# Two-layer attention and expert kernel: first attention's first diagonal chunk masked behind the exponentials instead of by mask products

## Chip, cores and metric

The kernel runs on one core of one Trainium2 chip. The metric is the time of one execution on the device, in microseconds (us); lower is better. The core's engines are named as in the profile: PE is TensorE, DVE is VectorE, ACT is ScalarE, POOL is GpSimd, SP is SyncE, which here only issues DMAs. PE, DVE, ACT and POOL each work through their own list of instructions in order and meet at semaphores.

## What is computed

The input x is 8 sequences of 256 tokens of 128 channels. Two blocks follow each other for every sequence:

```
x = layernorm(x + attention_A(x))           # 16 heads of 8 channels, one shared key and value head, rotary, causal
h = x + attention_B(rmsnorm(x, g1))         # 16 query heads of 64 channels, 4 key and value heads, rotary, causal
y = h + experts(rmsnorm(h, g2))             # router, top 2 of 8 experts, capacity limit
x = layernorm(x + y)
```

The change touches attention A. Its core, for one sequence:

```
att = einsum('bthd,bThd->bhtT', q, k) / sqrt(8)
att = where(T > t, -inf, att)               # a key later than the query counts nothing
att = softmax(att, axis=-1)
out = einsum('bhtT,bThd->bthd', att, v)
```

## The kernel before, in words

**Stages and steps.** Each sequence goes through eight stages (PA project A, MA row maxima A, SA scores and values A, TA finish A, PB project B, MB maxima B, SB scores and values B, TB finish B). The main loop runs steps s = -4 to 7. In a step each engine does one piece of every stage that is active, for different sequences: stage SA of sequence n is done in step s = n - 3 (`AHEAD`, L80), so SA is active in steps -3 to 4. PB is active in steps -2 to 5, SB from step 0, TB from step 1. The order of the work inside a step is written out by hand, once per engine: PE in `step` (L969), DVE in `step` (L1335), ACT in `step` (L1785), POOL in the loop at L586, the DMA issuer in the loop at L483. After the last step come the experts.

**PSUM.** Scores go to `ps_st` (two halves of 1024 columns). Everything else that PE makes goes through `ps_r`, a ring of four banks: PE takes the next bank with `fill` (L648), which waits until the reader of its previous content has freed it; the order is the list `ORDER` (L70).

**Scores of attention A.** The 256 x 256 causal square of a sequence is cut into three 128 x 128 chunks with keys on the partitions and queries along the row: DIAG0 (first keys, first queries), OFF, DIAG1. Each is done for all 16 heads, 2048 columns. `scores_a(s, c)` (L684) makes chunk c in four column groups of 512. For a diagonal chunk it first lays the mask into PSUM with four products of the identity and `kmask` (L696; -1e30 where the key is later than the query), then adds the four products of keys and queries (L699). Two exponentials on ACT (`exp_a`, L1684, the instruction at L1689) write the probabilities to `pt`: DIAG0 and DIAG1 to the same part, `pt_a(kind)` (L413), OFF to another. `values_a(s, qt)` (L704) multiplies probabilities and values (L714); `values_a(s, 0)` takes DIAG0 alone and waits for its two exponentials through `probs_a`. The row maximum that keeps the exponentials small comes from stage MA (masks at L661, products at L784, maxima on DVE at L1193, turned by PE at L791, negated by ACT at L1736, carried as a row by a DMA at L481); it is not touched.

**What stands around it in a step of PE:** B's projection `project(s, 0)` (L956), `scores_a(s, 0)`, A's maxima 10 and 11 (L661, L784), B's values (L929), the turned maxima (L791), B's weights (L945), B's maxima 8 to 11 (L661, L908), `project(s, 1)` (L956), the turned maxima of B (L916), A's input turned (L669), `values_a(s, 0)` (L714), `project_a` (L750, L755), the router's turned tokens (L812), `scores_a(s, 1)` (L699).

**DVE beside it:** B's rotary products of the first half, `rotate(s, 0)` (L1305 to L1309), A's maxima 10 and 11 (L1193), then, where TB is active, four small Newton steps for an inverse root (`newton`, L1155 to L1161) and two normalising products (L1392), B's maxima 8 to 11 (L1193), `rotate(s, 1)`, `rotate_a` (L1231 to L1239).

**POOL:** where TB is active two products on `oT` at the start of the step (L591), then `add_rotary(s, 0)` and `add_rotary(s, 1)` (three adds each, L554; each waits for DVE's bank to be freed, and DVE's later rotary writes wait for them), `spread_a` (L538 to L546), a copy of B's values (L610) and of the tokens (L621).

Of the kernel before, what the change touches and what calls it, by code (L numbers as in the profile page):

```python
# [27 lines left out]
ALU = mybir.AluOpType  # L28
# [3 lines left out]
P = 128  # L32
# [3 lines left out]
H = 16  # L36
# [25 lines left out]
DIAG0, OFF, DIAG1 = 0, 1, 2  # L62
# [17 lines left out]
AHEAD = {"PA": 4, "MA": 3, "SA": 3, "TA": 2, "PB": 2, "MB": 1, "SB": 0, "TB": -1}  # L80
# [10 lines left out]
def stages(step):  # L91

    return {x for x, a in AHEAD.items() if 0 <= step + a < NB}
# [82 lines left out]
E_A, E_B = len(CHUNKS_A), len(CHUNKS)  # L176
# [3 lines left out]
RG = P // 4  # L180
# [7 lines left out]
def build(nc, x, Wq, bq, Wk, bk, Wv, bv, Wo, bo, g1, g2, wq, wk, wv, wo, router_w, router_b,  # L188
          w1, w2, w3, cf, cb, out):
    with ExitStack() as ctx:  # L190
# [15 lines left out]
        def sem(name):  # L206
            return ctx.enter_context(nc.semaphore(name))
# [173 lines left out]
        free = [sem(f"free{b}") for b in range(RING.banks)]  # L381
        sc_a, sc_b = sem("sc_a"), sem("sc_b")
        probs_a, probs_b = sem("probs_a"), sem("probs_b")
        xn_in = sem("xn_in")
        prod_in = sem("prod_in")
        rot_in = sem("rot_in")
# [26 lines left out]
        def pt_a(kind):  # L413
            return pt[:, 2 + kind % 2]
# [12 lines left out]
        def emptied(eng, s, name):  # L427

            eng.wait_ge(free[RING.bank(s, name)], RING.freed(s, name) + 1)
# [89 lines left out]
        def _(pool):  # L519
# [13 lines left out]
            def spread_a(n):  # L533

                pool.wait_ge(chain_k, n + 1)
                both = qkr_a[:, :, 0:QA].rearrange("p t (h d) -> p t h d", d=DA)
                high = hr[:, :, :].bitcast(F32).rearrange("p t (h d) -> p t h d", d=DA)
                nc.gpsimd.tensor_tensor(qz[:, :, :, 2 * DA:3 * DA], both[:, :, 0:H, :], high[:, :, 0:H, :],  # L538
                                        ALU.subtract)
                for i in range(2):  # L540
                    nc.gpsimd.tensor_copy(qz[:, :, :, DA * i:DA * (i + 1)], high[:, :, 0:H, :])
                places = kz[:, :, :].rearrange("p t (a r) -> p t a r", a=4)
                one, hi_k = (x[:, :, H:, :].broadcast_to([P, NT, 4, DA]) for x in (both, high))
                for i in (0, 2):
                    nc.gpsimd.tensor_copy(places[:, :, :, DA * i:DA * (i + 1)], hi_k)
                nc.gpsimd.tensor_tensor(places[:, :, :, DA:2 * DA], one, hi_k, ALU.subtract).then_inc(kz_in, 1)  # L546

            def add_rotary(s, t):

                for i in range(3):  # L550
                    emptied(pool, s, f"p{t}{i}")
                    w = 512 if i < 2 else HKV * DB
                    part = qkr[:, t, 512 * i:512 * i + w]
                    nc.gpsimd.tensor_tensor(part, part, prod[:, (3 * t + i) % 2, 0:w], ALU.add).then_inc(add_in, 1)  # L554

            def scatter(i, lo, hi, src):

                pool.wait_ge(sc_in, i + 1)
                pool.wait_ge(z_dma, 48)
                for k in range(lo, hi):  # L560
                    if 1 < k < PASSES[0][1]:
                        pool.wait_ge(sc_dma[k % 2], 16 * (k // 2))
                    nc.gpsimd.indirect_dma_start(xs_dram[:, :], bass.IndirectOffsetOnAxis(sidx[:, k:k + 1], 0),
                                                 src[:, k - lo, :], None).then_inc(sc_dma[k % 2], 16)

            def load_slots(i):

                for a in range(2):
                    pool.wait_ge(sc_dma[a], 8 * PASSES[i][1])
                for k, (lo, hi) in enumerate(CHUNKS_X[i]):  # L570
                    nc.gpsimd.dma_start(xe[i][:, lo - START[i]:hi - START[i], :], rows(xs_dram, lo, hi)) \
                        .then_inc(xe_in[i][k], 16)

            def keep_inputs(lo, hi, src):

                for k in range(lo, hi):
                    ins = nc.gpsimd.tensor_tensor(src[:, k - lo, :], src[:, k - lo, :],
                                                  wx[:, k:k + 1].broadcast_to([P, C]), ALU.mult)
                ins.then_inc(keep_in, 1)
# [6 lines left out]
            for s in range(FIRST, NB):  # L586
                on, u, m = stages(s), s % 2, s - 1
                if "TB" in on:
                    pool.wait_ge(b_dma, 32 * s)
                    for k in range(HKV // 2):  # L590
                        ins = nc.gpsimd.tensor_tensor(  # L591
                            oT[:, k], pvb[1 - u][:, k, :, :].rearrange("p t (g c) -> p t g c", g=G), oT[:, k], ALU.mult)
                    ins.then_inc(oT_in, 1)
                if "PB" in on:
                    add_rotary(s, 0)
                    add_rotary(s, 1)
                if "PA" in on:
                    spread_a(s + AHEAD["PA"])
                if s == FIRST:
                    for z in range(2):  # L600
                        nc.gpsimd.memset(kdiag[z][:, :, :, :].bitcast(F32), 0.0).then_inc(zeroed, 1)
                    nc.gpsimd.memset(zeros, 0.0).then_inc(zx_in, 1)
                    pool.wait_ge(c_in, C_IN)
                    nc.gpsimd.tensor_copy(nrow[:, :, :].rearrange("p h (t c) -> p (h t) c", t=NT),
                                          kmask.unsqueeze(1).broadcast_to([P, H * NT, P])).then_inc(prep, 1)
                if "PB" in on:
                    pool.wait_ge(add_in, 6 * (s + 2) + 6)
                    if "SB" in on:
                        pool.wait_ge(full, RING.full(s, "sm1"))
                    nc.gpsimd.tensor_copy(vb[u][:, :, :, :].rearrange("p t k d -> p t (k d)"), qkr[:, :, QB:]) \  # L610
                        .then_inc(v_in, 1)
                if s == ROUTED[0]:
                    pool.wait_ge(xfa_in, NB0)
                    scatter(0, *PASSES[0], xf_all)
                    load_slots(0)
                if s == NB - 1:
                    pool.wait_ge(share_in, 1)
                    keep_inputs(*PASSES[0], xf_all)
                if "TB" in on:
                    pool.wait_ge(xf_in, m + 1)  # L620
                    nc.gpsimd.tensor_copy(xf_all[:, NT * m:NT * (m + 1), :], xf[:, :, :]).then_inc(xfa_in, 1)  # L621
# [23 lines left out]
        def _(pe):  # L645
# [38 lines left out]
            def scores_a(s, c):  # L684

                n = s + AHEAD["SA"]
                kind = KINDS_A[c]
                kt, qt = BLOCKS[kind]
                if n or c:
                    pe.wait_ge(probs_a, E_A * n + 2 * c)  # L690
                if c == 0 and s >= 0:
                    pe.wait_ge(probs_b, E_B * (s + 1))
                pe.wait_ge(r_dma[qt], 16 * (n + 1))
                o = [ps_st[:, a // 2, a % 2, :].rearrange("p (h t) -> p h t", h=4) for a in range(4)]
                for a in range(4) if kind != OFF else ():
                    nc.tensor.matmul(o[a], ident_b, kmask.unsqueeze(1).broadcast_to([P, 4, P]), start=True, stop=False)  # L696
                for a in range(4):
                    rows = slice(RG * a, RG * a + NROW + 1)
                    mm = nc.tensor.matmul(o[a], kta[rows, a, P * kt:P * (kt + 1)], qta[rows, :, P * qt:P * (qt + 1)],  # L699
                                          start=kind == OFF, stop=True, tile_position=(RG * a, 0))  # L700
                    if a % 2:
                        mm.then_inc(sc_a, 1)

            def values_a(s, qt):  # L704

                n = s + AHEAD["SA"]
                o = fill(s, f"av{qt}")
                if qt == 0:
                    emptied(pe, s - 1, "qkv")
                pe.wait_ge(probs_a, E_A * n + (2 if qt == 0 else E_A))  # L710
                blocks = [(DIAG0, 0)] if qt == 0 else [(OFF, 0), (DIAG1, 1)]
                for i, (kind, kt) in enumerate(blocks):
                    for a in range(4):
                        mm = nc.tensor.matmul(o[RG * a:RG * (a + 1), :], va[n % 2][:, kt, :],  # L714
                                              pt_a(kind)[:, 4 * a:4 * a + 4, :], start=i == 0,
                                              stop=i == len(blocks) - 1, tile_position=(0, RG * a))
                mm.then_inc(full, 1)
# [251 lines left out]
            def step(s):  # L969
# [51 lines left out]
                if "SA" in on:  # L1021
                    scores_a(s, 0)
# [26 lines left out]
                if "SA" in on:  # L1049
                    scores_a(s, 1)  # L1050
# [863 lines left out]
```

## Time and profile before

| what | value |
|---|---|
| median of 3 runs | 586.88 us (585.63 to 587.46) |
| profiled execution, its own time | 582.76 us |
| its span, first to last instruction | 580.9 us |
| PE busy | 483.3 us, 83% of the span |
| DVE busy | 386.6 us, 67% |
| ACT busy | 229.6 us, 40% |
| POOL busy | 161.6 us, 28% |
| mean granted TensorE clock | 0.940 of full speed |

Engine times are busy times and overlap each other. The rows further down come from the same profiled execution; their times count from the start of its span. In a row of the timeline the columns are the start in us, the duration in us (of all the instructions that the row merges), the engine, the line, the operation, output and inputs with their shapes, the count, and in brackets the idle time of the engine just before it with what ended it.

### The profile page before, as it was taken

The page shows a single profiled execution, that of the slowest core. Times are in us where ns is not written, and L with a number is a line of the kernel's source. Part 1 is how long each engine was busy: PE and PEld are TensorE (multiplying, and loading weights), DVE is VectorE, ACT ScalarE, POOL GpSimd, SP SyncE. Part 2 cuts the span into 40 slices and gives each one's busy share as a digit, 9 for nine tenths or more (in the row PEclk, how much of TensorE's full clock was granted, in tenths as well). Part 3 has the DMA queues.
Part 4 walks back from the last instruction along what each step waited for, and adds up shares of the span by engine and source line. Part 5 has one row for each costly group of instructions (what it writes and reads, how often), then busy time and mean ns, then how long its engine had stood idle before and what let it go on. Part 6 is the DMA issues. An engine that isn't in the chain of part 4 may idle for free.

```text
span 580.9 us, 8112 instructions
## 1 busy us (share of the span) xinstructions
PE 483.3 (83%) x2788; PEld 266.4 (46%) x2788; DVE 386.6 (67%) x1096; ACT 229.6 (40%) x420; POOL 161.6 (28%) x200
## 2 busy tenths in 40 slices
PE   3776886899989989998999899999878689898920
PEld 2333453454354535544563555355354336565610
DVE  3518879657758675777668576766877544675785
ACT  1241442454383346425432742464133132445400
POOL 4210602400413230324202330403406542043531
PEclk9877997899999999999999999999979899999965
DMA  7400000000011003000300030030070332023223
GB/s 210 156 1 2 2 0 1 3 1 1 3 38 38 1 4 75 1 1 3 73 2 2 3 73 3 2 74 1 15 207 20 101 77 73 2 60 100 70 54 86
DMA packets 19093, 23.82 MB, mean 41 GB/s; under 512 B 2630, under 2 KB 15374, under 8 KB 18158
## 3 DMA queue, kind: packets, MB, share of 16 engines
q1 hardware_dynamic: 15308, 18.19, 11.8%
q0 software_dynamic: 1648, 4.07, 2.5%
q10 hardware_dynamic: 2098, 1.05, 0.6%
q8 instruction: 23, 0.38, 0.3%
q14 instruction: 16, 0.13, 0.1%
HBM read 16.71 MB, written 6.28 MB: 40 GB/s over the span
## 4 chain that ended last, share of the span: by engine, by line
PE 57%; DVE 19%; ACT 11%; issue 5%; DMA 4%; POOL 3%; ACTq 1%; POOLq 0%; DVEq 0%; SPq 0%
PE ps_r L929 7%; PE ps_st L894 6%; ACT pt L1689 5%; PE ps_r L803 4%; PE ps_r L661 4%; PE ps_st L883 4%; PE ps_r L956 4%; DVE rmax L1193 3%; PE ps_r L714 3%; DMA pt<-ys_dram,gidx 3%; PE ps_r L945 3%; PE ps_r L784 3%; DVE rmax_a L1193 2%; POOL qkr L554 2%; PE ps_st L1095 2%
## 5 line engine op out<-in xcount | busy, mean ns | idle before, releaser
L554 POOL TENSOR_TENSOR qkr<-qkr,prod 128x512 f32<-128x512 f32 (+1 forms) x48 | 52.3, 1093 | 211.6 <-DVE prod L1309 210.6
L1193 DVE TENSOR_REDUCE rmax_a<-ps_r 128x2 f32<-128x512 f32 (+1 forms) x96 | 61.5, 685 | 20.6 <-PE ps_r L784 20.3
L1193 DVE TENSOR_REDUCE rmax<-ps_r 128x2 f32<-128x512 f32 (+1 forms) x96 | 61.1, 684 | 11.5 <-PE ps_r L908 10.2
L661 PE MATMUL ps_r<-cbt 128*128 128x256 bf16 (+1 forms) x192 | 63.1, 328 | 4.9 <-DVE rmax_a L1193 2.4
L1689 ACT ACTIVATE pt<-ps_st 128x1024 f32<-128x1024 f32 x48 | 46.5, 1022 | 44.5 <-PE ps_st L699 44.1
L1698 ACT ACTIVATE pt<-ps_st 128x1024 f32<-128x1024 f32 x48 | 47.2, 1022 | 39.6 <-PE ps_st L894 39.6
L591 POOL TENSOR_TENSOR oT<-pvb,oT 128x1024 f32<-128x1024 f32 x14 | 33.3, 2400 | 94.7 <-DMA oT<-inv_dram 94.7
L929 PE MATMUL ps_r<-pt,vb 128*64 128x512 f32 x192 | 48.5, 611 | 4.9 <-ACT pt L1698 3.2
L956 PE MATMUL ps_r<-wqkv,xT_b 128*128 128x512 f32 x96 | 45.9, 616 | 3.8 <-DVE rmax_a L1193 3.2
L784 PE MATMUL ps_r<-kq_a 128*128 128x512 f32 x96 | 45.7, 535 | 0.0
L661 PEld LDWEIGHTS ps_r<-cbt 128*128 128x128 bf16 x192 | 18.9, 99 | 48.7 <-issue 31.9
L894 PE MATMUL ps_st<-qbuf,kbuf 64*128 64x512 f32 x288 | 40.6, 414 | 0.0
L1321 DVE TENSOR_TENSOR qbuf<-ps_r,qbuf 128x512 fp32r<-128x512 f32 x32 | 20.8, 687 | 21.6 <-ACT qbuf L1773 21.6
L714 PE MATMUL ps_r<-pt,va 128*32 128x512 f32 x192 | 25.3, 630 | 10.8 <-ACT pt L1689 6.8
L1755 ACT ACTIVATE pvb<-ps_r 128x512 f32<-128x512 f32 x32 | 19.0, 594 | 37.1 <-PE ps_r L929 37.1
L894 PEld LDWEIGHTS ps_st<-qbuf,kbuf 64*128 64x128 f32 x288 | 25.9, 190 | 15.4 <-issue 11.0
L1306 DVE TENSOR_TENSOR qkr<-ps_r,cft 128x512 f32<-128x512 f32 (+1 forms) x48 | 28.5, 594 | 3.4 <-PE ps_r L956 3.4
L956 PEld LDWEIGHTS ps_r<-wqkv,xT_b 128*128 128x128 f32 x96 | 18.4, 200 | 22.1 <-issue 15.9
L883 PE MATMUL ps_st<-nrow,cbt 128*128 128x512 bf16 x96 | 26.5, 401 | 2.4 <-DMA nrow<-negmax 2.4
L908 PE MATMUL ps_r<-kbuf,qbuf 128*128 128x512 f32 x64 | 27.5, 502 | 0.0
L803 PE MATMUL ps_r<-wob,oT 128*128 128x128 f32 x224 | 26.4, 276 | 0.0
L803 PEld LDWEIGHTS ps_r<-wob,oT 128*128 128x128 f32 x224 | 25.6, 192 | 1.2 <-issue 1.2
(237 smaller groups left out, 901.1 us busy)
## 6 DMA issues: line engine op xcount, KB each, us to landing
oT<-inv_dram SPq DMA_DIRECT2D x14, 512.0 KB, 5.8
xs_dram<-pvb SPq DMA_DIRECT2D x1, 2048.0 KB
pt<-in_L_ffn_w SPq DMA_DIRECT2D x2, 1024.0 KB, 7.0
ys_dram<-qkr SPq DMA_DIRECT2D x14, 128.0 KB
qkr<-xs_dram POOLq DMA_DIRECT2D x4, 256.0 KB, 3.8
x_all<-in_L_attn_x ACTq DMA_DIRECT2D x1, 896.0 KB, 8.2
pvb<-xs_dram POOLq DMA_DIRECT2D x3, 256.0 KB, 4.3
out<-x_all SPq DMA_DIRECT2D x1, 640.0 KB, 3.8
```

The costliest lines, as they stand in the source:

```text
L554: nc.gpsimd.tensor_tensor(part, part, prod[:, (3 * t + i) % 2, 0:w], ALU.add).then_inc(add_in, 1)
L661: nc.tensor.matmul(o[:, :, P * (i >= 4):], ident_b, qmask.unsqueeze(1).broadcast_to([P, heads, P]), start=True, stop=False, skip_group_che ...
L714: mm = nc.tensor.matmul(o[RG * a:RG * (a + 1), :], va[n % 2][:, kt, :], pt_a(kind)[:, 4 * a:4 * a + 4, :], start=i == 0, stop=i == len(blo ...
L784: nc.tensor.matmul(o, q, k, start=False, stop=True, skip_group_check=True).then_inc(full, 1)
L803: mm = nc.tensor.matmul(o[:, 0:C], of, wob[:, j, :], start=j == 0, stop=j == H // 2 - 1)
L883: nc.tensor.matmul(o[b], top_row if kind == OFF else add_row, nrow[:, G * hk:G * (hk + 1), P * qt:P * (qt + 1)], start=True, stop=False)
L894: mm = nc.tensor.matmul(o[b], k, q, start=False, stop=ql, tile_position=(DB * b, 0))
L929: mm = nc.tensor.matmul(o[DB * b:DB * (b + 1), :], vb[s % 2][:, kt, hk, :], pt_b(kind)[:, G * hk:G * (hk + 1), :], start=j == 0, stop=j == ...
L956: nc.tensor.matmul(o, xT_b[:, P * t:P * (t + 1)], wqkv[:, 512 * i:512 * (i + 1)], start=True, stop=True).then_inc(full, 1)
L1193: nc.vector.tensor_reduce(heads_of(i), ps_r[:, b, :].rearrange("p (h k) -> p h k", h=4 if i < 4 else 2), AX.X, ALU.max).then_inc(free[b], 1)
L1689: nc.scalar.activation(pt_a(kind)[:, 8 * half:8 * half + 8, :], ps_st[:, c % 2, :, :].rearrange("p b (h t) -> p (b h) t", h=4), ACT.Exp, s ...
L1698: nc.scalar.activation(pt_b(kind)[:, 8 * half:8 * half + 8, :], ps_st[:, c % 2, :, :].rearrange("p b (h t) -> p (b h) t", h=4), ACT.Exp, s ...
```

## The change

For chunk DIAG0 of attention A the four mask products are left out: the score products start the sum in PSUM themselves. The exponentials are then taken of all 128 x 128 scores of a head. A new POOL function, `keep_causal`, waits for the two exponentials of DIAG0 and overwrites in place, over the 128 partitions and 2048 columns of `pt_a(DIAG0)`, every probability of a key later than the query with zero. In POOL's order it stands between `add_rotary(s, 0)` and `add_rotary(s, 1)`. `values_a(s, 0)` on PE waits for its new semaphore `causal_in` instead of for the exponentials. DIAG1 keeps its mask products, OFF never had any.

```diff
+        causal_in = sem("causal_in")
...
+            def keep_causal(s):
+
+                pool.wait_ge(probs_a, E_A * (s + AHEAD["SA"]) + 2)
+                probs = pt_a(DIAG0)
+                nc.gpsimd.affine_select(probs, probs, [[0, H], [1, P]], ALU.is_ge, 0.0, base=0, channel_multiplier=-1) \
+                    .then_inc(causal_in, 1)
+
...
                 if "PB" in on:
                     add_rotary(s, 0)
+                if "SA" in on:
+                    keep_causal(s)
+                if "PB" in on:
                     add_rotary(s, 1)
...
-                for a in range(4) if kind != OFF else ():
+                for a in range(4) if kind == DIAG1 else ():
                     nc.tensor.matmul(o[a], ident_b, kmask.unsqueeze(1).broadcast_to([P, 4, P]), start=True, stop=False)
                 for a in range(4):
                     rows = slice(RG * a, RG * a + NROW + 1)
                     mm = nc.tensor.matmul(o[a], kta[rows, a, P * kt:P * (kt + 1)], qta[rows, :, P * qt:P * (qt + 1)],
-                                          start=kind == OFF, stop=True, tile_position=(RG * a, 0))
+                                          start=kind != DIAG1, stop=True, tile_position=(RG * a, 0))
...
-                pe.wait_ge(probs_a, E_A * n + (2 if qt == 0 else E_A))
+                if qt == 0:
+                    pe.wait_ge(causal_in, n + 1)
+                else:
+                    pe.wait_ge(probs_a, E_A * (n + 1))
```

## Rows read from the trace of the kernel before

**Rows 1.** The page's first and fourth part: busy time, and the chain by engine.

```profile
PE 483.3 (83%) x2788; PEld 266.4 (46%) x2788; DVE 386.6 (67%) x1096; ACT 229.6 (40%) x420; POOL 161.6 (28%) x200
...
PE 57%; DVE 19%; ACT 11%; issue 5%; DMA 4%; POOL 3%; ACTq 1%; POOLq 0%; DVEq 0%; SPq 0%
```

**Rows 2.** The chain that ended last, step 1: start us, us on the chain, what.

```profile
200.01 0.86 PE ps_st L696 x4
...
202.12 1.87 PE ps_r L929 x8
...
204.05 0.27 PE ps_r L791
...
209.06 0.68 DVE qkr L1306
```

**Rows 3.** DVE's timeline, step 1.

```profile
202.62 1.28 DVE L1193 TENSOR_REDUCE rmax_a<-ps_r 128x2 f32<-128x512 f32 x2
203.82 0.15 DVE L1155 TENSOR_TENSOR root_t_a<-root_t_r 128x2 f32<-128x2 f32 x1
...
204.60 0.61 DVE L1392 SCALAR_TENSOR_TENSOR xf<-y,root_t_r,g2b 128x128 f32<-128x128 f32 x2
...
206.66 2.49 DVE L1193 TENSOR_REDUCE rmax<-ps_r 128x2 f32<-128x512 f32 x4 [1.44 <-PE ps_r L908]
```

**Rows 4.** The same handoff in step -2: DVE's last maxima and PE's next instruction.

```profile
61.77 1.28 DVE L1193 TENSOR_REDUCE rmax_a<-ps_r 128x2 f32<-128x512 f32 x2
63.19 0.27 PE L791 MATMUL ps_r<-cft,rmax_a 128*16 128x128 f32 x1 [1.51 <-DVE rmax_a L1193]
```

**Rows 5.** Timeline of POOL, ACT and PE around the new instruction's place, step 1.

```profile
200.18 3.34 POOL L554 TENSOR_TENSOR qkr<-qkr,prod 128x512 f32<-128x512 f32 x3 [17.33 <-DVE prod L1309]
...
201.34 1.94 ACT L1689 ACTIVATE pt<-ps_st 128x1024 f32<-128x1024 f32 x2 [4.42 <-PE ps_st L699]
...
210.48 3.32 POOL L554 TENSOR_TENSOR qkr<-qkr,prod 128x512 f32<-128x512 f32 x3 [6.96 <-DVE prod L1309]
...
211.71 1.07 PE L714 MATMUL ps_r<-pt,va 128*32 128x512 f32 x8 [0.82 <-DVE prod L1309]
```

**Rows 6.** POOL by line and form: count, busy us, mean ns of one, idle before.

```profile
L554 POOL TENSOR_TENSOR qkr<-qkr,prod 128x512 f32<-128x512 f32 x32 | 40.6, 1276 | 210.2 <-DVE prod L1309 210.2
L591 POOL TENSOR_TENSOR oT<-pvb,oT 128x1024 f32<-128x1024 f32 x14 | 33.3, 2400 | 94.7 <-DMA oT<-inv_dram 94.7
...
L610 POOL COPY vb<-qkr 128x512 f32<-128x512 f32 x8 | 4.9, 608 | 0.1
```

**Rows 7.** Timeline: Newton instructions of DVE with and without a POOL product beside.

```profile
132.06 0.15 DVE L1155 TENSOR_TENSOR root_a_a<-root_a_r 128x2 f32<-128x2 f32 x1
...
178.17 4.68 POOL L591 TENSOR_TENSOR oT<-pvb,oT 128x1024 f32<-128x1024 f32 x2 [13.72 <-DMA oT<-inv_dram]
...
181.67 1.20 DVE L1155 TENSOR_TENSOR root_a_a<-root_a_r 128x2 f32<-128x2 f32 x1
...
408.85 3.33 POOL L554 TENSOR_TENSOR qkr<-qkr,prod 128x512 f32<-128x512 f32 x3 [11.36 <-DVE prod L1309]
...
411.48 0.72 DVE L1157 TENSOR_TENSOR root_t_a<-root_t_a,root_t_v 128x2 f32<-128x2 f32 x1
```

**Rows 8.** Timeline of step -3, the first with stage SA.

```profile
23.63 1.89 PE L696 MATMUL ps_st<-cbt 128*128 128x512 bf16 x4 [0.74 <-DMA kq_a<-nega]
...
26.28 1.94 ACT L1689 ACTIVATE pt<-ps_st 128x1024 f32<-128x1024 f32 x2 [4.53 <-PE ps_st L699]
...
28.89 1.06 PE L714 MATMUL ps_r<-pt,va 128*32 128x512 f32 x8
```

**Rows 9.** POOL's timeline, step -2.

```profile
65.79 3.34 POOL L554 TENSOR_TENSOR qkr<-qkr,prod 128x512 f32<-128x512 f32 x3 [3.14 <-DVE prod L1309]
```

**Rows 10.** Stretches: us, busy (x) of PE, PEld, DVE, ACT, POOL, clock, DMA.

```profile
60.00:68.00 8.00, 6.49 (x34) 2.79 (x31) 6.30 (x17) 3.19 (x5) 4.81 (x5) 1.00 0.00 1
...
198.00:206.00 8.00, 7.94 (x42) 2.56 (x40) 6.88 (x20) 2.68 (x4) 3.27 (x3) 1.00 0.00 0
```

## Prediction

> **What bounds the kernel now.** The page comes first. PE is busy 83% of the span, DVE 67%, POOL 28%, and the chain that ended last lies on PE for 57% and on DVE for 19% [rows 1]. From that alone, 32 mask products fewer on PE look like a plain gain. The chain of one step says more. In step 1 the four mask products of DIAG0 are on it with 0.86 us, and so is everything of PE behind them up to 204.05, where PE turns the row maxima at L791 [rows 2]. This instruction needs more than PE: it waits until DVE has reduced A's maxima 10 and 11. DVE does so from 202.62 to 203.90 [rows 3], and L791 starts at 204.05, 0.15 later. Is 0.15 us simply how long the handoff takes? Step -2 tells it: there PE stood idle 1.51 us in front of L791, for certain waiting on DVE, which ended at 63.05; L791 started at 63.19, 0.14 later [rows 4]. So in step 1 PE's own work ended (202.12 to 203.99) just as DVE's did, and L791 is bound by both at once. DVE's work in front of 203.90 is the rotary of the first half, released by L956 and not by the mask products. The chain program picks one of two parents; the other forbids the gain.
>
> Behind L791 PE works alone for 2.6 us, DVE idles 1.44 us, then starts B's maxima 8 to 11 at 206.66 [rows 3]. From here DVE goes without a gap into the rotary of the second half at 209.06 [rows 2], and PE, POOL and `values_a(s, 0)` hang on its freed banks (0.82 us of idle in front of L714, released by DVE) [rows 5]. Whatever makes DVE late at 206.66 makes the step longer, one for one.
>
> **The change, part by part.** I call the duration of the new POOL instruction X.
>
> *Mask products out, steps 0 to 4.* 0.86 us each on PE. Gain: 0, since L791 stays at DVE's 203.90 plus 0.15. If DVE were not there it would be 5 x 0.86 = 4.3 us. Steps -2 and -1 gain 0 too: L791 has its 1.51 us of idle in step -2 [rows 4], and step -1 has the same order of work without B's values.
>
> *X itself.* No row shows this operation on POOL. It reads one tensor and writes one, 2048 columns. Lower bound: a copy. 512 columns take 0.61 us [rows 6]; with nothing but the row scaled by four it is 2.4, but part of each instruction is fixed; the 1024 and 512 columns of the two-input products (2.40 and 1.28 [rows 6]) show 1.12 for the second 512, so a fixed part of about 0.15. A copy of 2048 is then 0.15 + 4 x 0.46 = 2.0 us. Upper bound: a two-input product, 0.15 + 4 x 1.12 = 4.6 us. By its traffic it is nearest to the copy; but it works out a position, compares and selects for each element, where a copy does nothing. I take 2.6 us, the copy plus a quarter of the way, and keep 2.0 and 4.6 for the range. The Trainium skill, GPSIMD Engine Reference, Performance pitfalls for Q7 kernels, gives a loop that compares and selects 1.03 to 2.03 cycles per element, which at its 1.2 GHz would be estimates of 1.8 and 3.5 us; the sum below would be about -0.5 and +7.8 by them.
>
> *When it runs, steps 1 to 4.* POOL's three adds end at 203.52 [rows 5]; the exponentials end at 203.28 now and 0.86 earlier then, so they don't decide. POOL is then idle for 6.96 us until 210.48, and PE wants the probabilities at 211.71 [rows 5]. With X = 2.6 it ends at 206.1. Neither POOL nor PE waits for it; what is queued behind it, the adds of the second half, is 4 us away. On these two engines it is free up to X = 6.9.
>
> *What it does to DVE.* A Newton product on two columns takes 0.15 us. Beside POOL's products it took 1.20: started at 181.67, ended 182.87, where POOL's pair ended at 182.85. Another took 0.72 and ended at 412.20, where POOL's adds ended at 412.18 [rows 7]. The instruction is held until POOL's instruction is over. The first of four of the same family starts at 203.82 in step 1 [rows 3], 0.3 us into the new instruction. It would be held to 203.52 + X + 0.02. From its end (203.97) to the end of L1392 (205.21) are 1.24 us, and a following instruction of DVE overlaps its predecessor by 0.08 (203.82 against 203.90) [rows 3]. So DVE can begin B's maxima at 203.54 + X + 1.16 = 204.70 + X, instead of 206.66. It is late by X - 1.96: 0.64 us for 2.6; 0.04 for 2.0; 2.64 for 4.6. Steps 1 to 4 have this pattern (TB and SA both active), so 4 x 0.64 = +2.6 us. Step 0 has no Newton there. That a POOL instruction with one input holds DVE as one with two does is not in any row: not held, this term is 0. I take it as held, since both groups of POOL's products hold DVE to their very end, and the new instruction reads the same memory. The Trainium skill, SBUF — State Buffer, Who interferes with whom, says that a DVE instruction with two SBUF inputs contends with any GpSimd instruction that reads SBUF, and that the loser waits for the whole instruction. By that rule the term is +2.6, without it 0.
>
> *Step -3.* Here nothing else is near. The masks start at 23.63, on the chain, and the exponentials end at 28.22 [rows 8]. Without masks, 1.89 us less a small overlap, everything is 1.8 us earlier and the exponentials end at 26.4. POOL is idle. With 0.2 us for the two handoffs (0.15 is the one of rows 4), `values_a` starts at 26.6 + X instead of at 28.89 [rows 8]. Change: X - 2.3 = +0.3 us; -0.3 and +2.3 at the ends.
>
> *Step -2.* POOL is free from 62.65 to 65.79, 3.14 us [rows 9]. X = 2.6 hides; X = 4.6 costs 1.5. Step -1 has, as steps 0 to 4, B's maxima 8 to 11 on PE between the two groups of adds, and room of that size.
>
> **Sum.** 0 + 2.6 + 0.3 = +2.9 us; at X = 2.0 it is 0.2 - 0.3 = -0.1; at X = 4.6 it is 10.6 + 2.3 + 1.5 = +14.4. Against the profiled execution, 582.76 becomes 585.7. The median of the runs stands 4.1 us above it, so 586.88 + 2.9 = 589.8 us, 0.5% slower. About 0.3%, 1.8 us, is what a measurement of this kernel can tell from no change.
>
> **Rivals.**
> 1. *All of it hides.* DVE isn't held by a one-input instruction, or X is near the copy. Only step -3 moves, by -0.3 to +1, and X may be up to 3.1 without more: 586.6 to 588. For it: POOL's long idle. Against it: rows 7, and that X has to be below 2.4 where the hold is real (4 x 0.44 is the 1.8 us). Chance 0.33.
> 2. *PE gets its 0.86 us.* L791 in steps 0 to 4 in truth waits for PE's last product, and nothing is held: 586.88 - 4.3 + 0.3 = 582.9. For it: the chain names PE. Against it: the same 0.15 us of handoff where PE was surely waiting. It is decided by DVE's 203.90; were the rotary a microsecond shorter it would be so. Chance 0.06.
> 3. *The clock.* From 60 to 68 PE is busy 6.49 of 8 us at the full clock [rows 10]; without the masks it is 5.6, and PE's idle in front of L791 grows to 2.4. If the clock falls to its half behind that, it costs up to a microsecond or two in steps -3 and -2. From 198 to 206 PE is busy 7.94 of 8 [rows 10], so 0.9 less leaves the clock there alone. It adds to the others and turns none.
> 4. *X beyond 4.6.* +14.4 and more; from 6.9 on POOL's adds wait in every step. Chance 0.05.
>
> The change can't fail to do what it says: the 32 products are gone from PE's list.
>
> **Numbers.** The forecast, held and X from 2.4 to 4.6, has 0.56. Slower by over 0.3%: 0.56 + 0.05, less a little for its lower edge, 0.59; within: 0.35; faster: 0.06. The range reaches from rival 1's lower end, 586.5, to X = 4.3, 600; below lies rival 2, above the rest of X. The forecast's own range is 588.7 to 601.
>
> **What would show it.** L696 with 32 products instead of 64. L791 in step 1 still 0.15 behind DVE's reduction, with about 0.9 us of idle in front of it now: right on the first step; at 203.2 it would be wrong. The new instruction at 203.5 with its X. The first Newton product of steps 1 to 4 as long as to the end of it, in place of 0.15; if it still takes 0.15, the hold is wrong and rival 1 stands. DVE's idle in front of B's maxima gone from 1.44 to nothing, the step longer by X - 1.96. `values_a` in step -3 directly behind POOL, elsewhere still behind DVE's banks. X below 2.4 would make the forecast wrong even with all the rest right.

## The result, and the profile after

The kernel after takes 593.62 us in the median of 8 runs (590.87 to 597.46), beside 587.66 us for the kernel before in 8 runs (585.26 to 590.11): a ratio of 1.0102, 95% interval 1.0072 to 1.0132. It is slower. Two repeats gave 1.0128 and 1.0110 (below), so 6 to 7.5 us is the size to explain. The profiled execution of after, 597.46 us with a span of 595.6, was the slowest of its 8, and that of before, 582.76, was quicker than any of its 8. The two traces differ by 14.7 us and can't be subtracted as they stand. Every stage is therefore read on its own, and in more than one trace.

The page of after, its first and fourth part (before: [rows 1]):

```profile
PE 482.8 (81%) x2756; PEld 264.8 (44%) x2756; DVE 392.7 (66%) x1096; ACT 230.1 (39%) x420; POOL 177.0 (30%) x208
...
PE 44%; DVE 28%; ACT 11%; issue 5%; DMA 5%; POOL 4%; another core or an unknown queue 1%; ACTq 1%; POOLq 0%; DVEq 0%; SPq 0%
```

The 32 products and their 32 weight loads are gone (2788 to 2756), and PE is busy for only 0.5 us less. The products before had cost far more than that (four of them 0.86 us in step 1, [rows 2]), so others of PE's instructions must have become longer. That is the first trace of the clock.

The new instruction on POOL, by line and form (count, busy us, mean ns of one, idle before):

```profile
L561 POOL TENSOR_SCALAR_AFFINE_SELECT pt<-pt 128x2048 f32<-128x2048 f32 x8 | 16.0, 2005 | 9.3 <-ACT pt L1703 9.3
```

X, the duration of the new instruction, is 2.0 us: the price that the prediction worked out for a copy, and nothing for the comparison. The timeline of after, step 1, with all engines, answers to [rows 2], [rows 3] and [rows 5]:

```profile
208.11 1.28 DVE L1207 TENSOR_REDUCE rmax_a<-ps_r 128x2 f32<-128x512 f32 x2
...
208.95 2.00 POOL L561 TENSOR_SCALAR_AFFINE_SELECT pt<-pt 128x2048 f32<-128x2048 f32 x1
209.30 1.66 DVE L1169 TENSOR_TENSOR root_t_a<-root_t_r 128x2 f32<-128x2 f32 x1
...
209.53 0.27 PE L805 MATMUL ps_r<-cft,rmax_a 128*16 128x128 f32 x1 [0.71 <-DVE rmax_a L1207]
...
212.15 2.49 DVE L1207 TENSOR_REDUCE rmax<-ps_r 128x2 f32<-128x512 f32 x4
...
215.98 2.52 POOL L555 TENSOR_TENSOR qkr<-qkr,prod 128x512 f32<-128x512 f32 x2 [5.03 <-DVE prod L1323]
```

Three things are to be seen. PE turns the maxima 0.14 us behind DVE's reduction (209.39 to 209.53), as before, and now stands idle 0.71 us in front of it: PE's gain from the missing products lies in that idle. The Newton product, 0.15 us before, takes 1.66 and ends at 210.96, as the select does at 210.95: a POOL instruction with one input holds DVE too. And DVE goes into B's maxima without its 1.44 us of idle. From the first reduction to B's maxima it is 4.04 us in both kernels (208.11 to 212.15; 202.62 to 206.66 in [rows 3]). The hold fills the idle and costs nothing.

Step -3 is where the values now wait, PE, ACT and POOL of after (before: [rows 8]):

```profile
25.38 0.51 PE L710 MATMUL ps_st<-kq_a 25*128 25x512 f32 x4 [1.11 <-DMA kq_a<-nega]
...
25.91 1.94 ACT L1703 ACTIVATE pt<-ps_st 128x1024 f32<-128x1024 f32 x2 [2.42 <-PE ps_st L710]
...
27.81 0.27 PE L805 MATMUL ps_r<-cft,rmax_a 128*16 128x128 f32 x1 [1.11 <-DVE rmax_a L1207]
...
27.93 2.00 POOL L561 TENSOR_SCALAR_AFFINE_SELECT pt<-pt 128x2048 f32<-128x2048 f32 x1 [9.29 <-ACT pt L1703]
...
30.08 1.94 PE L728 MATMUL ps_r<-pt,va 128*32 128x512 f32 x8 [1.77 <-POOL pt L561]
...
36.37 1.89 PE L707 MATMUL ps_st<-cbt 128*128 128x512 bf16 x4 [2.03 <-ACT pt L1703]
...
41.10 3.64 PE L728 MATMUL ps_r<-pt,va 128*32 128x512 f32 x16 [2.12 <-ACT pt L1703]
```

The first values take 1.94 us in place of 1.06: PE runs at its half clock from here, and goes on so to the second values. The mean granted clock from 20 to 50 us (columns: stretch, us, PE busy, clock, DMA share, GB/s), first after, then before:

```profile
20.00:50.00 30.00, 21.55 (x101) 0.72 0.08 30
```

```profile
20.00:50.00 30.00, 21.85 (x115) 0.83 0.09 31
```

A mean of 0.72 over 30 us, from levels of 1 and 0.5, is 16.8 us at the half clock; 0.83 is 10.2.

One more difference shows where each step begins, by the first of B's scores. PE in after, then in before, at the starts of steps 1 and 2:

```profile
174.16 0.81 PE L897 MATMUL ps_st<-nrow,cbt 128*128 128x512 bf16 x3
...
229.49 0.81 PE L897 MATMUL ps_st<-nrow,cbt 128*128 128x512 bf16 x3
```

```profile
169.86 0.81 PE L883 MATMUL ps_st<-nrow,cbt 128*128 128x512 bf16 x3
...
223.99 0.81 PE L883 MATMUL ps_st<-nrow,cbt 128*128 128x512 bf16 x3
```

Step 1 lasts 55.33 us against 54.13. The extra 1.2 us arise at the step's beginning, far from the select. SP stores the inverted sums (16 KB) and loads them back spread out, and POOL and `project_out` hang on that. The DMA view over the life of this store, after (173.9 to 176.6), then before (169.6 to 171.1):

```profile
q8 instruction: 1, 0.02, 2.6%
q1 hardware_dynamic: 48, 0.02, 2.6%
...
inv_dram<-sums SPq DMA_DIRECT2D x1, 16.0 KB, 2.6
```

```profile
q1 hardware_dynamic: 48, 0.02, 4.2%
...
inv_dram<-sums SPq DMA_DIRECT2D x1, 16.0 KB, 1.4
```

In after 16 KB of program (queue q8, of the kind "instruction") are fetched inside this stretch and the store takes 2.6 us; in before none are, and it takes 1.4. The trace doesn't say whose program it is. PE's has 64 instructions fewer now, so its fetches would fall at other moments. That was a guess at this point, as was the weight of the clock.

### The profile page after: what moved, and what is told of

Read it like the earlier page. It is cut to its first block, busy times and chain, and to the rows that moved or that the text cites. A ratio compares the mean times of both kernels' runs of the same rounds, so it can differ in the third digit from the quotient of the medians.

```text
span 595.6 us, 8057 instructions
## 1 busy us (share of the span) xinstructions
PE 482.8 (81%) x2756; PEld 264.8 (44%) x2756; DVE 392.7 (66%) x1096; ACT 230.1 (39%) x420; POOL 177.0 (30%) x208
## 3 DMA queue, kind: packets, MB, share of 16 engines
HBM read 16.71 MB, written 6.28 MB: 39 GB/s over the span
## 4 chain that ended last, share of the span: by engine, by line
PE 44%; DVE 28%; ACT 11%; issue 5%; DMA 5%; POOL 4%; another core or an unknown queue 1%; ACTq 1%; POOLq 0%; DVEq 0%; SPq 0%
ACT pt L1703 6%; PE ps_st L908 5%; PE ps_r L943 5%; DVE rmax L1207 5%; PE ps_r L817 4%; DVE rmax_a L1207 4%; PE ps_r L728 3%; PE ps_st L897 3%; PE ps_r L672 3%; DMA pt<-ys_dram,gidx 3%; POOL qkr L555 3%; DVE qkr L1320 2%; PE ps_r L798 2%; PE ps_st L1109 2%; PE ps_r L778 2%
## 5 line engine op out<-in xcount | busy, mean ns | idle before, releaser
L970 PE MATMUL ps_r<-wqkv,xT_b 128*128 128x512 f32 x96 | 47.9, 638 | 3.8 <-DVE rmax_a L1207 3.2
L798 PE MATMUL ps_r<-kq_a 128*128 128x512 f32 x96 | 46.9, 548 | 0.0
L728 PE MATMUL ps_r<-pt,va 128*32 128x512 f32 x192 | 26.5, 657 | 12.2 <-ACT pt L1703 6.8
L1261 DVE RECIPROCAL rda<-ps_r 128x16 f32<-128x16 f32 x16 | 4.0, 253 | 34.5 <-PE ps_r L741 34.5
```

The lines of the kernel that those rows point to most:

```text
L798: nc.tensor.matmul(o, q, k, start=False, stop=True, skip_group_check=True).then_inc(full, 1)
L970: nc.tensor.matmul(o, xT_b[:, P * t:P * (t + 1)], wqkv[:, 512 * i:512 * (i + 1)], start=True, stop=True).then_inc(full, 1)
```

## The experiments

Theory A of the first four runs had one cause: in step -3 the wait for the select lets the clock fall. After them it had two, neither of them the hold: that one, and that the shortened program of PE moves its fetches onto small transfers. The rival (theory C in the first runs): the selects themselves cost it, by the hold on DVE or by the wait for them in every step. Theory B is a loss in the late steps.

| kernel | ratio to before, 95% interval | steps -3 to -1 | step 1 | steps 2 to 4 | step 5 to end | store | clock 20 to 50 |
|---|---|---|---|---|---|---|---|
| before | 1 | 103.1 | 54.13 | 158.6 | 198.3 | 1.4 | 0.83 |
| before again | 1.0017 (0.9983 to 1.0050) | 102.6 | 54.13 | 158.6 | 199.0 | 1.4 | 0.89 |
| after | 1.0102 (1.0072 to 1.0132) | 107.3 | 55.33 | 159.0 | 207.1 | 2.6 | 0.72 |
| after, second | 1.0128 (1.0094 to 1.0161) | 105.2 | 55.46 | 158.7 | 202.4 | 3.0 | 0.72 |
| after, third | 1.0110 (1.0073 to 1.0147) | 105.5 | 54.77 | 159.1 | 201.4 | 2.4 | 0.72 |
| sequences 1 to 7 only | 1.0071 (1.0039 to 1.0102) | 103.2 | 55.26 | 158.7 | 202.5 | 2.4 | 0.83 |
| sequence 0 only | 1.0071 (1.0039 to 1.0102) | 106.0 | 54.14 | 158.6 | 198.4 | 1.4 | 0.72 |
| masks and select | 1.0095 (1.0058 to 1.0132) | 105.7 | 54.13 | 158.6 | 198.9 | 1.4 | 0.77 |
| neither | 1.0048 (1.0015 to 1.0081) | 103.5 | 54.94 | 159.6 | 198.8 | 2.6 | 0.83 |
| select twice | 1.0264 (1.0220 to 1.0307) | 108.0 | 56.38 | 164.5 | 196.9 | 2.4 | 0.77 |
| after, PE padded | 1.0109 (1.0065 to 1.0152) | 107.2 | 54.15 | 158.6 | 199.3 | 1.4 | 0.72 |
| sequences 1 to 7, padded | 1.0011 (0.9983 to 1.0038) | 103.7 | 54.14 | 158.9 | 199.1 | 1.4 | 0.89 |
| after, fillers | 1.0084 (1.0046 to 1.0122) | 104.0 | 54.14 | 158.6 | 195.4 | 1.4 | 0.89 |
| after, fillers and padding | 1.0037 (1.0008 to 1.0067) | 104.0 | 54.33 | 158.7 | 195.7 | 1.4 | 0.89 |

The ratios come from all runs, the other columns (us) from one trace each: from A's first maxima to step 0's first scores, then between the starts of B's scores as read above, and the store's time to landing. The kernels below ran in three groups, the first on one chip and the other two on another, each group beside its own runs of the kernel before. Their ratios can be compared, though not to the last digit: on the second chip the median of the kernel before itself went from 580.23 us in one group to 582.41 in the next, 0.4%. And a trace is one execution: that of "after, fillers", 580.80 us, was the quickest of its nine, whose median is 586.17.

**Repeats.** The kernels before and after, unchanged.

> The kernel before, unchanged, for a second trace. Every theory: ratio 1.000 within 0.3%. What it adds is how far two traces of one kernel lie apart, stretch by stretch. If the clock in steps -4 to -2 falls at other times than in the first trace, the start alone can move by 2 us or more without any change.

> The changed kernel, unchanged, for a second trace. Every theory: 1.007 to 1.013 of before. Theory A (the clock in step -3): from the landing of the row of maxima to the last product of values in step -3 it is again about 2 to 3 us longer than before, at half the granted clock. Theory B (the late steps): the loss behind 450 us, 8.8 of the 14.7 us between the first two traces, is there again. If neither is there again, both were chance of one trace.

> The kernel after once more, on the chip on which the next three run, as their measure. Both theories: ratio 1.010 to 1.013, step 1 (start of step 1's second-attention scores to step 2's) 55.3 us, the first step of the pipeline (first maxima of step -3 to the first scores of step 0) 105 to 107 us against 103 before.

The loss is real. Step 1 was 55.46 and 54.77, with the store at 3.0 and 2.4 us, and the part behind the start of step 5, 207.1 us in the first trace, was 202.4 and 201.4 beside 198.3 and 199.0 before: theory B's loss is there again, at less than half.

**Split by sequence.** In the first kernel sequence 0 keeps its mask products and has no select; in the second only sequence 0 is changed. Here and below only the telling lines of an edit are shown; start flags and waits are changed to fit.

```
-                for a in range(4) if kind == DIAG1 else ():
+                for a in range(4) if kind == DIAG1 or (kind == DIAG0 and n == 0) else ():
...
-                if "SA" in on:
+                if "SA" in on and s > FIRST + 1:
                     keep_causal(s)
```

> The change for sequences 1 to 7 alone; sequence 0 (step -3) keeps its mask products and has no new wait. Theory A (step -3 and its clock carry the loss): most of the 6 us are gone, ratio 1.000 to 1.003. Theory C (DVE held by the new instruction in steps 1 to 4 carries it): still 1.007 or more. By the traces so far C has only 0.02 us a step at the maxima, and 1.2 us once in step 1 where two other holds of DVE fell otherwise.

> The change for sequence 0 alone, in step -3; steps -2 to 4 keep their mask products and have no new instruction. Theory A: 1.006 to 1.010, nearly all of the loss, with the clock at half behind the new wait. Theory C: within 0.3% of before.

Each half costs 0.7%. For the second kernel that is what theory A expected. For the first it isn't: 1.000 to 1.003 was expected, and 1.0071 is what theory C gave, so the ratio alone spoke for the hold. The stages speak against it. With sequence 0 alone the loss is in the first stages (106.0), with the seven others it is in step 1 (55.26) and behind step 5. Steps 2 to 4, with a select in each, are as long as before: no loss by the hold.

**Masks against select.** The first kernel has both for DIAG0, the second neither: it leaves out that chunk's scores and mask, for with scale 0 its probabilities are all one.

```
-                for a in range(4) if kind == DIAG1 else ():
+                for a in range(4) if kind != OFF else ():
```

```
-                if "SA" in on:
-                    keep_causal(s)
...
+                                     ACT.Exp, scale=0.0 if kind == DIAG0 else DA ** -0.5).then_inc(probs_a, 1)
```

> The mask products are kept and GpSimd's select is added behind them; nothing is left out. Theory A: TensorE's program keeps its old length, so step 1 lasts 54.1 us and the part behind step 5 is about 198 to 199 us; step -3 costs more than before by 2 to 4 us, since the values wait for the select; ratio about 1.005 (1.003 to 1.009). Rival (the selects cost it in every step): ratio 1.010 to 1.014, step 1 at 55.3 us.

> Neither mask products nor select for the first diagonal chunk; its exponentials are taken at scale 0, so its probabilities are all one and its later keys are not zeroed: what is left out is that chunk's scores and mask. Theory A: no wait for a select, so step -3 is as before or up to 0.9 us shorter, but TensorE's program is shorter as in the kernel after: step 1 at 55.3 us and the part behind step 5 at 202 us or more; ratio about 1.006 to 1.010. Rival (the selects cost it): ratio 0.998 to 1.002, step 1 at 54.1 us or less.

Up to step 5 both came out as theory A has it: with the masks kept step 1 is 54.13 although the select is there, and with neither it is 54.94 with a store of 2.6 us although no select is. In the kernel with neither step 3 is long too, 55.19 us against 54.13 to 54.42 in eleven of the thirteen other traces, again with a store of 2.6 us and a fetch in it. But its part behind the start of step 5 is 198.8 us, where theory A wanted 202 or more: a short program of PE doesn't by itself make that part long. And both ratios lie between the two theories: 1.0095 where theory A ended at 1.009 and the rival began at 1.010, 1.0048 where they said 1.006 or more and 1.002 or less. The kernel with neither has something to show of its own. PE in its step -3:

```profile
24.82 0.50 PE L708 MATMUL ps_st<-kq_a 25*128 25x512 f32 x4 [0.75 <-DMA kq_a<-nega]
...
27.68 1.94 PE L723 MATMUL ps_r<-pt,va 128*32 128x512 f32 x8
...
31.10 0.51 PE L708 MATMUL ps_st<-kq_a 25*128 25x512 f32 x4
```

Its values start 2.86 us behind the first scores. With masks at the full clock it is 3.82 (the padded kernel below, 25.32 to 29.14). But they take 1.94 us at the half clock, and the next scores come 6.28 us behind the first, where with masks it is 5.85 (25.32 to 31.17). In this trace the 1 us that the products take is given back with interest. That they had been part of the work that kept PE at its full clock is argued from one trace, and isn't the whole: in the first trace of the kernel before the masks themselves ran at the half clock [rows 8].

**Dose of the hold.** Each select twice, the second waiting for the first.

```
+                pool.wait_ge(causal_in, 2 * (s + AHEAD["SA"]) + 1)
+                nc.gpsimd.affine_select(probs, probs, [[0, H], [1, P]], ALU.is_ge, 0.0, base=0, channel_multiplier=-1) \
+                    .then_inc(causal_in, 1)
```

> The kernel after with each select made twice, the second waiting for the first; the result is the same. It doubles the time for which GpSimd's instruction may hold VectorE's Newton products and for which the first values of step -3 wait. Hold theory (the prediction's, X minus 1.96 a step): with X at 4.0 us in place of 2.0 the steps 1 to 4 each last 2.0 us longer than in the kernel after, step -3 2.0 us, in sum +8 to +10 us, ratio about 1.025. Rival (the hold is not on the path, the loss is elsewhere): at most +2 us for step -3, ratio 1.010 to 1.016.

DVE and POOL in step 1 of this kernel:

```profile
208.95 2.00 POOL L561 TENSOR_SCALAR_AFFINE_SELECT pt<-pt 128x2048 f32<-128x2048 f32 x1
209.30 1.67 DVE L1172 TENSOR_TENSOR root_t_a<-root_t_r 128x2 f32<-128x2 f32 x1
...
211.03 2.01 POOL L564 TENSOR_SCALAR_AFFINE_SELECT pt<-pt 128x2048 f32<-128x2048 f32 x1
211.20 1.86 DVE L1176 TENSOR_SCALAR root_t_a<-root_t_a 128x2 f32<-128x2 f32 x1
...
213.82 2.48 DVE L1210 TENSOR_REDUCE rmax<-ps_r 128x2 f32<-128x512 f32 x4
```

B's maxima begin at 213.82 in place of 212.15 in after, with the first select at 208.95 in both: 1.67 us later for 2.08 us more of POOL, since one Newton instruction slips in between the two selects. Steps 2 to 4 last 5.9 us longer than in the padded kernel, of which 0.9 is step 3's, whose store takes 2.4 us with a fetch in it; and the ratio, 1.0264, is the 1.025 of the hold theory. So the prediction's mechanism is real, 1.7 us a step here, and with X = 2.0 the kernel sits just at its edge. By the Trainium skill, SBUF — State Buffer, Who interferes with whom, a reduction never contends with GpSimd on this chip, while a `tensor_scalar` in its two-port mode does; the rows agree: the reduction beside the select keeps its 1.28 us, and L1176, a `tensor_scalar`, takes 1.86, though no row shows its mode.

**Padding.** 16 waits that are always met, which come to 8 instructions, in the place of each step's mask products, so that PE's program has its old length.

```
+                for _ in range(16) if kind == DIAG0 else ():
+                    pe.wait_ge(id_in, 16)
```

> The kernel after, with 16 waits that are always met put into TensorE's program in each stage where the mask products were, so that its program has its old length again (8 fewer instructions a stage in the kernel after). Nothing is left out. Theory A (the loss is step -3's later values with the lower granted clock, about +3 us, and the rest comes of the instruction fetches of TensorE's program, which moved onto small transfers such as the store of the sums): the store of the sums in step 1 takes 1.4 us again in place of 2.6, step 1 lasts 54.1 us in place of 55.3, the part behind the start of step 5 lasts 198 to 199 us in place of 202 to 207, and the ratio to the kernel before is about 1.005 (1.003 to 1.008). Rival (the selects themselves cost it, by holding VectorE or by the wait for them): nothing changes against the kernel after, ratio 1.010 to 1.013.

The starts of steps 1 and 2, and the store, of this kernel:

```profile
173.97 0.81 PE L899 MATMUL ps_st<-nrow,cbt 128*128 128x512 bf16 x3
...
228.12 0.81 PE L899 MATMUL ps_st<-nrow,cbt 128*128 128x512 bf16 x3
```

```profile
q1 hardware_dynamic: 48, 0.02, 3.5%
...
inv_dram<-sums SPq DMA_DIRECT2D x1, 16.0 KB, 1.4
```

Step 1 is back at 54.15 and the store at 1.4 us with no fetch in its stretch, by instructions that do nothing. That is theory A's stage as foretold. The ratio isn't: 1.0109 where 1.005 was expected, the interval leaves 1.005 out, and the rival's 1.010 to 1.013 holds it. All of this kernel's trace but the first stages is as before (5.1 us in all, 4.0 of them up to step 0). That is 0.9%, inside the interval; but its runs show no gain over the kernel after, and an interval of 1.0065 to 1.0152 can't say how large a gain it would miss. So padding was tried without the clock's part.

> Sequence 0 (step -3) with its mask products and no select, sequences 1 to 7 as in the kernel after with TensorE's program padded to its old length. Nothing is left out. Theory A (two causes, step -3 with its clock and the shifted instruction fetches): neither is left, so every step has its length of before and the ratio is 0.998 to 1.003. Rival (the selects of the sequences 1 to 7 cost of themselves): 1.005 to 1.010, as without the padding (1.007).

This is the split kernel "sequences 1 to 7" with padding from sequence 1 on. 1.0011: no loss is left, with seven selects in place, against 1.0071 without the padding; the intervals (0.9983 to 1.0038 and 1.0039 to 1.0102) just miss each other. A cost of the seven selects above 0.4% is refuted. And it shows that seven eighths of the change, cleared of both troubles, gain nothing either: none of the kernels tried is faster than the one before.

**The clock.** Eight matmuls of the mask into the bank of the first values, in step -3, ahead of the wait; the values overwrite them. The second kernel is padded as well, from sequence 2 on, since the eight fill up the length of two stages.

```
+                if n == 0 and qt == 0:
+                    for _ in range(8):
+                        nc.tensor.matmul(o.rearrange("p (h t) -> p h t", h=4), ident_b,
+                                         kmask.unsqueeze(1).broadcast_to([P, 4, P]), start=True, stop=True)
                 if qt == 0:
                     pe.wait_ge(causal_in, n + 1)
```

> The kernel after with 8 matmuls of the mask into the bank of the first values in step -3 alone, ahead of the wait for the select; their result is overwritten, and nothing is left out. Theory A (the clock): TensorE has work in the wait of 1.8 us, so the stretch at the lower clock between 26 and 46 us is shorter than 17 us (about 7 to 9 us, as before), and the time from the first maxima of step -3 to step 0 falls from 105 to 107 us to 103 to 105 us; ratio 1.006 to 1.010. Rival (only the wait itself costs it there, not the clock): no change against the kernel after, 105 to 107 us and 1.010 to 1.013.

> The kernel after with both: the 8 filling matmuls in step -3 and TensorE's program padded to its old length. Nothing is left out. Theory A: what is left is the wait of step -3 itself, at most 2 us: ratio 1.001 to 1.005. Rival (the selects cost it in every step, the clock is no cause): 1.008 to 1.013.

PE in step -3 with fillers (and padding), and its clock:

```profile
25.33 0.51 PE L712 MATMUL ps_st<-kq_a 25*128 25x512 f32 x4 [1.05 <-DMA kq_a<-nega]
...
28.09 1.89 PE L725 MATMUL ps_r<-cbt 128*128 128x512 bf16 x8
29.93 1.06 PE L734 MATMUL ps_r<-pt,va 128*32 128x512 f32 x8
...
31.79 0.51 PE L712 MATMUL ps_st<-kq_a 25*128 25x512 f32 x4
...
37.92 3.64 PE L734 MATMUL ps_r<-pt,va 128*32 128x512 f32 x16 [2.12 <-ACT pt L1709]
```

```profile
20.00:50.00 30.00, 22.96 (x125) 0.89 0.08 29
```

The first values start just when they did in after (29.93 and 30.08), so the wait is the same. The fillers only keep PE at work through it, and the values take 1.06 us again, the second values start at 37.92 in place of 41.10, and the stretch at the half clock shrinks to 6.6 us. The time up to step 0 falls from 107.2 (padded, no fillers) to 104.0 us, but the kernel after alone has 105.2 to 107.3 there, so the price of the clock is better read from a shorter stretch. From PE's first product of step -3's scores to its second values it is 15.7 us in all five traces with one select in step -3, no masks and no fillers (after three times, "sequence 0 only", padded), and 12.6 us in both with fillers: the clock's price is 3.1 us. The two ratios, 1.0084 and 1.0037, are inside what was expected. 1.0084 isn't told apart from the kernel after in the same group, 1.0110; 1.0037 (1.0008 to 1.0067) against 1.0109 (1.0065 to 1.0152) of the padded kernel, in another group, is, if only just: the intervals touch.

For the wait itself, the padded kernel with masks in step -3 gives the measure, with PE's first instruction at nearly the same time:

```profile
25.32 1.04 PE L709 MATMUL ps_st<-cbt 128*128 128x512 bf16 x4 [1.05 <-DMA kq_a<-nega]
26.29 0.51 PE L712 MATMUL ps_st<-kq_a 25*128 25x512 f32 x4
...
29.14 1.06 PE L730 MATMUL ps_r<-pt,va 128*32 128x512 f32 x8
...
37.29 3.64 PE L730 MATMUL ps_r<-pt,va 128*32 128x512 f32 x16 [2.11 <-ACT pt L1705]
```

From the first instruction to the values it is 3.82 us with masks and 4.60 with the select: the wait costs 0.8 us, of which 0.6 reach the second values (11.97 us behind the first instruction with masks, 12.59 with the select).

**What stays open.** Behind the start of step 5 the kernels with one select in sequences 1 to 7, PE's short program and no fillers took 201.4 to 207.1 us in four traces, the padded ones 195.7 to 199.3, but the short-program kernels "neither", "select twice" and "fillers" 195.4 to 198.8. Three of the four, and none of the other ten traces, show a stall that the profile puts down to "remote", another core or an unknown queue, beside POOL's indirect scatters: of DVE and ACT in after (3.38 and 5.04 us) and in "sequences 1 to 7 only" (1.06 and 3.61), of DVE in the second run of after. After, then its second run:

```profile
462.50 2.67 DVE L1207 TENSOR_REDUCE rmax<-ps_r 128x2 f32<-128x512 f32 x4 [3.38 <-remote]
```

```profile
458.44 0.29 DVE L1457 TENSOR_TENSOR y<-ps_r,x_all 128x128 f32<-128x128 f32 x1 [5.41 <-remote]
```

The third run of after has no such row and is still at 201.4. No run isolates this part, and its cause isn't settled. Nor is it explained why the padded kernel's runs show no gain over the kernel after.

## Why the prediction was right or wrong, by its steps

The forecast was slower, 589.8 us; the median is 593.62, inside the range, and the sign is right. Both are luck. The 2.9 us forecast were almost all the hold on DVE, which cost nothing; of the 6 us measured the sum had only the wait in step -3, with the wrong sign at the measured X. The clock stood outside the sum as rival 3, and the fetches were not thought of.

- **Mask products out, gain 0: right.** PE turns the maxima 0.14 us behind DVE, and 0.71 us of new idle stands before it. That PE could gain 0.86 us a step (rival 2) is refuted.
- **X: mis-sized.** Taken as 2.6 us, measured 2.0, the lower bound. The quarter of the way to the product, for comparison and selection, had no row behind it.
- **The hold on DVE in steps 1 to 4: right in mechanism, its size nothing.** The product is held to the select's end, as foretold. At X = 2.0 the prediction's own formula gives 0.04 us a step in place of 0.64, and steps 2 to 4 of the padded kernel last 158.6 us as before. The double select brings the term back, at 1.7 us a step where the formula, with 4.0 in place of 2.0, would add 2.0. So "+2.6" failed wholly by X, and with it the main term of the sum.
- **Step -3, X - 2.3: mis-sized.** The step took the masks' saving as 1.8 us from a row of 1.89 [rows 8], which was at the half clock. At the full clock four products take 1.04 us (the row at 25.32 above), and the exponentials end only 0.97 us earlier (28.77 and 27.80 in the two kernels compared last). Instead of -0.3 at X = 2.0 the wait costs +0.8. Against the traced execution the formula does hold: there the values came 5.26 us behind the first product, and in after 4.70.
- **Rival 3, the clock: right place and sign, too small.** "Up to a microsecond or two" was 3.1 us, and the sum left it out. It was argued from step -2; the fall comes in step -3, where PE stands idle 1.11 us for DVE, works 0.5 us and stands idle 1.77 us for POOL.
- **The length of PE's program: not foreseen.** The prediction counted what the 32 products cost on PE's array, and not that 64 instructions fewer move every later fetch. It costs 1.2 us in step 1 of the kernel after (1.3 and 0.6 in its other traces), shown by padding; in the ratios 0.6% in the pair without the clock's part, and nothing that can be measured in the other.
- **Not held, PE or DVE ahead of all (rival 1):** of its two grounds the first is refuted (DVE is held) and the second was true: X was near the copy, and the hold hid. Its time of 586.6 to 588 was missed by what it didn't look at, the clock and the store.

The sum as measured: 0.6 for the wait and 3.1 for the clock, together 3.7, where "sequence 0 only" costs 0.7% or 4.1 us; 1.2 in step 1; and the remainder to 6 us, about 1, is put down to the part behind step 5, whose cause is open.

## What to carry to other kernels

Matmuls that nobody waits for can be what keeps TensorE's clock up, as the fillers did here: before one is taken out or a wait put in, look for the stretches in which the granted clock is already below 1 at times, and take the prices of the instructions there from rows at the same clock. A term of the form "X minus a slack" wants X measured by itself first, because a small error in X turns it from nothing into the main loss. After any change of an instruction count compare the step lengths, and if one moved that has nothing to do with the edit, pad the program back to its old length before looking for a deeper cause.

## What the runs showed that was not expected

- GpSimd's select by position, 128x2048 in f32, takes 2.00 us, the rate of its copy (512 columns in 0.61 us [rows 6]).
- The half clock came behind gaps of only 1.11 and 1.77 us with a little work between, and then lasted: 16.8 us of the 30 from 20 to 50, against 6.6 to 10.2 without the wait. It doesn't grow with the gap: with the select twice PE stood idle 3.86 us and the half clock came to 13.8. 1.9 us of matmuls with no use took the excess away.
- A 16 KB fetch of program inside the life of a 16 KB store made it last 2.4 to 3.0 us in six of six traces in step 1, where it takes 1.4 in the eight others. In step 3 it was so in three traces ("after, third", "neither", "select twice"; 2.3 to 2.6 us), and the first two of them have a step 3 of 54.67 and 55.19 us. The kernel before isn't free of it: in its second trace the store of step 5 took 2.2 us with a fetch in it, and 1.4 in the first without.
- By chance the traces of one and the same kernel differ early as well, again by the clock. Before's masks of step -3 began at 23.63 us in one and 25.01 in the other; PE's first mask product for A's maxima (L661) had taken 0.38 us in the one and 0.58 in the other. After's first scores began at 25.38, 23.34 and 23.58. A single pair of traces can't give a loss of this size.
